# Attention and routed experts on one core: partition sums in four column tiles with a block transpose, and the causal mask as a select on GpSimd

## The reference, cut to what matters

```
q, k, v = (x @ w.T) reshaped to heads            # 16 heads, 128 wide
q, k = rmsnorm(q, q_norm_w), rmsnorm(k, k_norm_w) # x * rsqrt(mean(x*x) + 1e-6) * w
q, k = apply_rope(q), apply_rope(k)
scores = 50 * tanh(q @ k.T / sqrt(128) / 50)
scores = where(mask above the diagonal, -inf, scores)
attn = softmax(scores)
x = layernorm(x + (attn @ v) @ wo.T)
x = layernorm(x + moe(x))                         # 32 experts, 6 per token, and a shared one
```

## Time and profile before

| | |
|---|---|
| runs | 1281.82, 1280.22, 1281.23 us; median 1281.23 |
| profiled execution, span from first to last instruction | 1275.8 us |
| what lies around the span (median less span) | 5.4 us |
| TensorE, VectorE, ScalarE, GpSimd busy over the span | 1137.5, 1077.5, 700.1, 745.7 us |
| mean granted TensorE clock | 0.976 of full speed |
| one step of the attention, mean of 31 | 30.26 us |

### The profile page before, as it was taken

The page is one execution under the profiler, slowest core; times in us unless marked ns, Lnnn a source line. Parts: engine busy times, 40 slices in busy tenths (PEclk is TensorE's granted clock), DMA queues, the critical chain, the costliest instruction groups (busy, mean ns, idle before and its releaser), DMA issues.

```text
span 1275.8 us, 21790 instructions
## 1 busy us (share of the span) xinstructions
PE 1137.5 (89%) x6879; PEld 963.6 (76%) x6879; DVE 1077.5 (84%) x1683; ACT 700.1 (55%) x1143; POOL 745.7 (58%) x665
## 2 busy tenths in 40 slices
PE   4699999989999999999999999999988878499998
PEld 3578788878888887888888888788877753277788
DVE  5599999999999999999999999999999669814654
ACT  2466666666666666666666666666666523022210
POOL 2366767676666666676667676767677536170001
PEclk9799999999999999999999999999999879799999
DMA  4000100000000000000000011100000070017911
GB/s 149 26 31 25 47 21 29 21 29 21 29 25 25 25 25 25 25 25 25 25 25 25 25 32 33 33 21 29 21 21 17 1 237 1 0 50 199 240 33 54
DMA packets 42142, 55.67 MB, mean 44 GB/s; under 512 B 8864, under 2 KB 34816, under 8 KB 42112
## 3 DMA queue, kind: packets, MB, share of 16 engines
q1 hardware_dynamic: 36336, 49.49, 12.8%
q10 hardware_dynamic: 5200, 4.22, 1.2%
q0 software_dynamic: 576, 1.57, 0.4%
HBM read 49.37 MB, written 4.33 MB: 42 GB/s over the span
## 4 chain that ended last, share of the span: by engine, by line
PE 33%; POOL 26%; DVE 22%; issue 11%; ACT 5%; DMA 2%; POOLq 1%; SPq 0%; DVEq 0%; ACTq 0%
POOL rstd L870 10%; POOL pacc L891 9%; PE ps L358 7%; POOL praw L881 6%; PE ps L360 6%; PE ps L359 6%; DVE qraw L1098 6%; DVE qhat_lo L1015 5%; PE ps L615 3%; PE ps L623 2%; ACT praw L711 2%; DVE qhat_hi L1025 2%; ACT prob_hi L672 2%; PE ps L640 2%; PE ps L641 2%
## 5 line engine op out<-in xcount | busy, mean ns | idle before, releaser
L881 POOL TENSOR_TENSOR praw<-praw,causal 128x128 f32<-128x128 f32 x256 | 211.9, 828 | 236.8 <-ACT praw L711 236.8
L672 ACT ACTIVATE prob_hi<-praw 128x1024 fp32r<-128x1024 f32 (+7 forms) x256 | 171.3, 683 | 216.6 <-POOL praw L881 216.5
L1015 DVE TENSOR_TENSOR prob_lo<-praw,prob_hi 128x1024 fp32r<-128x1024 f32 (+7 forms) x256 | 256.1, 1020 | 38.0 <-ACT prob_hi L672 36.8
L891 POOL TENSOR_TENSOR pacc<-pacc,praw 128x768 f32<-128x768 f32 (+2 forms) x192 | 239.3, 1247 | 28.5 <-POOL praw L881 26.6
L358 PE MATMUL ps<-qhat_hi,kT_hi 128*128 128x512 f32 (+3 forms) x384 | 144.6, 376 | 66.5 <-DVE qhat_lo L1015 42.7
L705 ACT ACTIVATE praw<-ps,rstd 128x1024 f32<-128x1024 f32 (+7 forms) x256 | 182.8, 735 | 11.8 <-PE ps L360 3.0
L711 ACT ACTIVATE praw<-praw 128x1024 f32<-128x1024 f32 (+7 forms) x256 | 163.4, 677 | 0.0
L870 POOL TENSOR_TENSOR rstd<-var,mhalf 128x16 f32<-128x16 f32 x32 | 125.3, 3915 | 60.7 <-DVE var L1053 60.7
L358 PEld LDWEIGHTS ps<-qhat_hi,kT_hi 128*128 128x128 f32 x384 | 73.4, 191 | 93.3 <-issue 40.3
L358 PE MATMUL ps<-prob_hi,vS_hi 128*128 128x512 f32 (+3 forms) x384 | 136.5, 355 | 2.6 <-DVE prob_lo L1015 2.5
L360 PE MATMUL ps<-qhat_hi,kT_lo 128*128 128x512 f32 (+3 forms) x384 | 134.0, 349 | 0.0
(11 more groups left out here) (170 smaller groups left out, 2516.7 us busy)
## 6 DMA issues: line engine op xcount, KB each, us to landing
rqB<-rq_rows SPq DMA_DIRECT2D x32, 512.0 KB, 3.7
wgu<-in_wgu SPq DMA_DIRECT2D x32, 352.0 KB
wd<-in_wd SPq DMA_DIRECT2D x32, 176.0 KB
wraw<-in_wqkv SPq DMA_DIRECT2D x16, 256.0 KB, 3.6
wv<-in_wqkv SPq DMA_DIRECT2D x16, 128.0 KB, 2.1
woraw<-in_wo SPq DMA_DIRECT2D x16, 128.0 KB, 2.0
yacc<-in_x SPq DMA_DIRECT2D x1, 2048.0 KB, 13.9
x_rows<-yacc SPq DMA_DIRECT2D x2, 1024.0 KB, 8.6
```

The source lines that it names most:

```text
L672: return nc.scalar.activation(dst, src, ACT.Copy)
L881: nc.gpsimd.tensor_tensor(diag, diag, causal[:, :], ALU.mult).then_inc(mask_done, 1)
L891: nc.gpsimd.tensor_tensor(pacc[:, b, P * j:T], before, raw, ALU.add).then_inc(pacc_done, 1)
L1015: v.tensor_tensor(dst, x_, hi.bitcast(F32), ALU.subtract).then_inc(done, 1)
```

## The change

The squares are no longer reduced on VectorE before the matmul. TensorE multiplies them as the moving operand with a 128 x 32 stationary operand of ones, 256 columns at a time, in four column tiles of 32 columns: tile g takes the 32-token strips g, g+4, g+8 and so on, and writes PSUM partitions 32g to 32g+31, all 32 rows alike. VectorE then transposes the bank in 32 x 32 blocks, after which column 0 of each block holds 32 tokens' sums down the partitions, and one instruction makes `var` of it. The denominators are made in the same way from `pacc`: four matmuls of 256 columns in place of eight loads of `pacc`, all at one place behind scores 3, and a transpose of 128 x 256 ahead of the reciprocal. `rstd` now has token 128 j + p at (p, j), so the q half is written to DRAM element by element, 4 bytes each. The mask is an `affine_select` in place on the diagonal block. Some constants go or move to the routed part.

```
-                mm(ps[:, bank_no, 0:2 * BLK * TT], fold[:, :], sqp[:, :, :, :].rearrange("p m g j -> p (m g j)"),
-                   start=True, stop=True).then_inc(pj_done, 1)
+            def strip_sums(bank_no, c0, by_strip):
+                for g in range(BLK):
+                    last = mm(ps[32 * g:32 * g + 32, bank_no, c0:c0 + 32 * TT].rearrange("p (j r) -> p j r", r=32), ones[:, :],
+                              by_strip[:, g], start=True, stop=True, tile_position=(0, 32 * g))
+                return last
+            def strips(row):
+                return row.rearrange("p (j g r) -> p g j r", g=BLK, r=32)
...
+                pe.wait_ge(qsq_done, step + 1)
+                strip_sums(bank_no, 0, strips(qsq[:, :]))
+                pe.wait_ge(ksq_done, step * 2 + 2)
+                strip_sums(bank_no, 32 * TT, strips(ksq[:, :])).then_inc(pj_done, 1)
...
+                strip_sums(bank_no, 0, strips(pacc[:, b, :])).then_inc(pj_done, 1)
...
-                sp.dma_start(rq_d[b].rearrange("(p j) -> p j", p=P), rstd[:, b, 0:TT]).then_inc(rq_out, 16)
+                sp.dma_start(rq_d[b].rearrange("(j p) -> p j", p=P), rstd[:, b, 0:TT], allow_slow_non_contiguous=True).then_inc(rq_out, 16)
...
-                nc.gpsimd.tensor_tensor(diag, diag, causal[:, :], ALU.mult).then_inc(mask_done, 1)
+                nc.gpsimd.affine_select(out=diag, in_=diag, compare_op=ALU.is_ge, fill=0.0, base=0,
+                                        pattern=[[1, P]], channel_multiplier=-1).then_inc(mask_done, 1)
...
-                    for g in range(BLK):
...
-                    last.then_inc(pj_free, 1)
+                    v.transpose(sqT[:, :], bank).then_inc(folded, 1)
+                    dve.wait_ge(folded, step + 1)
+                    v.tensor_scalar(var[:, b, :], sqT[:, :].rearrange("p (n r) -> p n r", r=32)[:, :, 0],
+                                    1.0 / DH, RMS_EPS, ALU.mult, ALU.add).then_inc(pj_free, 1)
...
-                v.reciprocal(rsum[:, b, :], ps[:, bank_no, 0:TT]).then_inc(pj_free, 1)
+                v.transpose(sumT[:, :], ps[:, bank_no, 0:32 * TT]).then_inc(pj_free, 1)
+                dve.wait_ge(pj_free, count)
+                v.reciprocal(rsum[:, b, :], sumT[:, :].rearrange("p (j r) -> p j r", r=32)[:, :, 0]).then_inc(rsum_done, 1)
```

More of the change, by code:

```diff
@@ L413, in values, with sums @@
                 last.then_inc(pv_done, 1)
-            def sums(s, b, half, count, bank_no):
-                if half == 0:
-                    open_unit(count)
-                    pe.wait_ge(pacc_done, (s + 1) * TT + RING)
-                for j in range(TT // 2 * half, TT // 2 * half + TT // 2):
-                    last = mm(ps[:, bank_no, j:j + 1], pacc[:, b, P * j:P * j + P], ones[:, 0:1], start=True, stop=True)
-                if half == 1:
-                    last.then_inc(pj_done, 1)
+            def sums(s, b, count, bank_no):
+                open_unit(count)
+                pe.wait_ge(pacc_done, (s + 1) * TT + RING)
+                strip_sums(bank_no, 0, strips(pacc[:, b, :])).then_inc(pj_done, 1)
             def out_proj(s, b, u, count, bank_no):
@@ L470, in step @@
                     values(s - 1, 1 - b, 7)
-                    sums(s - 1, 1 - b, 0, *hd.unit(b, "sums"))
                 scores(s, b, 2)
@@ L474, in step @@
                 if old:
-                    sums(s - 1, 1 - b, 1, *hd.unit(b, "sums"))
+                    sums(s - 1, 1 - b, *hd.unit(b, "sums"))
                     if b == 1:
@@ L512, in _ @@
                 values(s - 1, 1, j)
-            for half in range(2):
-                sums(s - 1, 1, half, *end.unit(0, "sums"))
+            sums(s - 1, 1, *end.unit(0, "sums"))
             for u in range(4):
@@ L676, in _, with squares_free, projected @@
                 copy_hi(xT[0][:, :, b * T:b * T + T], xraw[:, :, b * T:b * T + T]).then_inc(xhi_done, 1)
-            def projected(what, b, count, bank_no):
+            def squares_free(step):
+                if not (isinstance(step, int) and step == 0):
+                    act.wait_ge(folded, step)
+            def projected(what, b, step, count, bank_no):
                 if what == "q":
+                    squares_free(step)
                     act.wait_ge(pj_free, count)
@@ L854, in _ @@
             for row, col, value in ((0, 1, 1.0), (1, 1, float(P)), (2, 2, 1.0)):
[L855 removed]
+                pool.wait_ge(consts, 6 + row)
                 nc.gpsimd.affine_select(out=rest[:, col:col + 1], in_=rest[:, col:col + 1], compare_op=ALU.not_equal, fill=value,
                                  base=-row, pattern=[[0, 1]], channel_multiplier=1).then_inc(consts, 1)
[L858 to L863 removed]
             pool.wait_ge(consts, CONSTS)
@@ L1050, in projected @@
                 if what == "ss":
-                    for g in range(BLK):
-                        rows = slice(32 * g, 32 * g + 32)
-                        last = v.tensor_scalar(var[rows, b, :].rearrange("p (m j) -> p m j", m=2),
-                                               bank[rows, 0:2 * BLK * TT].rearrange("p (m g j) -> p m g j", m=2, g=BLK)[:, :, g, :],
-                                               1.0 / DH, RMS_EPS, ALU.mult, ALU.add)
-                    last.then_inc(pj_free, 1)
+                    v.transpose(sqT[:, :], bank).then_inc(folded, 1)
+                    dve.wait_ge(folded, step + 1)
+                    v.tensor_scalar(var[:, b, :], sqT[:, :].rearrange("p (n r) -> p n r", r=32)[:, :, 0],
+                                    1.0 / DH, RMS_EPS, ALU.mult, ALU.add).then_inc(pj_free, 1)
                     return
@@ L1116, in tile, with out_projected @@
                 lo_of(prob[1][:, j % RING, 0:n], praw[:, j % RING, 0:n], prob[0][:, j % RING, 0:n], plo_done)
-            def out_projected(b, u, sums_count, count, bank_no):
+            def out_projected(b, u, step, count, bank_no):
                 if u == 0:
-                    dve.wait_ge(pj_free, sums_count)
+                    dve.wait_ge(rsum_done, step + 1)
                 dve.wait_ge(pj_done, count)
@@ L1160, in step @@
                     tile(s - 1, 6)
-                if new:
-                    fold_squares(s + 1, 0)
                 if old:
@@ L1173, in step @@
                     output_lo(s - 1)
-                if new:
-                    fold_squares(s + 1, 3)
                 if old:
                     summed(1 - b, *hd.unit(b, "sums"))
-                    out_projected(1 - b, 0, hd.unit(b, "sums")[0], *hd.unit(b, "op0"))
+                    out_projected(1 - b, 0, s - 1, *hd.unit(b, "op0"))
                 if new:
@@ L1182, in step @@
                 if old:
[L1183 removed]
+                    out_projected(1 - b, 1, s - 1, *hd.unit(b, "op1"))
                 tile(s, 1)
@@ L1244, in _ @@
             for u in range(4):
-                out_projected(1, u, end.unit(0, "sums")[0], *end.unit(0, f"op{u}"))
+                out_projected(1, u, s - 1, *end.unit(0, f"op{u}"))
             dve.wait_ge(pj_free, UNITS_ALL)
```

102 lines of the change are left out of this document (30 added, 72 removed).

## The result

The changed kernel takes 1546.61 us (median of 4 runs, 1541.71 to 1547.61), the kernel before 1280.72 (1279.32 to 1281.82, 4 runs) on the same chip: a ratio of 1.206, 95% interval 1.2025 to 1.2098. The forecast was 1287, the range 1243 to 1358. It is slower, as the likeliest case said, but by 266 us where that case had 6, and beyond the range.

A forecast was written before the change was run, and what follows sets the result against it. A latency loop of TensorE, VectorE's var, GpSimd's power and a three-engine tail bounds the kernel: 0.63 - 0.45 = +0.18 us a step, times 31 is +5.6, from 1275.8 to 1281.4, plus 5.4 gives 1287 us; range 1243 to 1358.

The forecast's parts named there:

- the likeliest case: Whole kernel: slower, chance 0.59 in all; the main forecast, chance 0.45, had +0.18 us a step, +5.6 us.
- The transfer: Write of rstd's q half in 1024 packets of 4 bytes: 0.5 us more taken, other bound 10 us; costs nothing.
- the row on packets: Profile's view of transfers: 144 packets at 4.6% of 16 engines over 1.7 us, 8.7 ns each.
- the 1.8 that were free: Slack in us before q's scaling needs the transferred row, after GpSimd's gain from the masks.
- Rival C: 4-byte packets become the bound: from some 37 ns each slack is gone, 60 ns adds 62 us, 1349; chance 0.10.
- the 2.2 that were free: Slack in us between the row's landing at about 585.1 and q's scaling making progress at 587.35.
- The wait ahead of the denominators: TensorE's wait of 0.64 us for a bank VectorE has not yet read, predicted to go.
- The middle way of 5 and 9 passes: TensorE's column-tile matmuls overlap partly: denominators 1.08 us, squares 1.94, plus 0.1 a group; squares end 0.56 later.
- rival A: All four column tiles run at once on TensorE: squares end 0.71 earlier, step 1.09 us shorter, 1247 us; chance 0.20.
- VectorE's part: Squares' end to var 0.17 us longer, 0.1 back on average; the net 5.9 us saved counted at nothing.
- GpSimd's part: Affine select for the mask product: 0.45 us off a step over four masks, bounds 0.16 to 0.64.
- B: Rival: column tiles on TensorE take turns, squares end 2.73 later, +2.35 us a step, 73 us, 1354; chance 0.25.

The follow-up runs named there:

- e1_fixed: The changed kernel with the q half of rstd written in whole 32-byte pieces, q's strips read at a step of 8: 1253.33 us, ratio 0.979.
- e4_product: e1_fixed with the causal mask as a product on GpSimd again instead of the affine select: 1275.59 us, ratio 0.996.
- e12_ss_values7: e1_fixed with the squares' sums on TensorE moved from behind scores 4 to behind values 7, their VectorE transpose also earlier: 1188.28 us, ratio 0.927.
- e9_in_turn: e1_fixed without column tiles, the same strip matmuls each over all 128 columns, keeping only the last strip's sums: 1395.48 us, ratio 1.091.
- e13_order_alone: The kernel before with the affine select, VectorE's fold kept, squares' sums moved behind scores 3, last fold and variances earlier: 1375.14 us, ratio 1.072.

## Why the prediction was wrong, point by point

**The transfer: the step that failed.** I had two bounds for the write: 8.7 ns a packet, from the engines' share, hence +0.5 us, and 175 ns for each of 56 more, from the 1.4 us to landing, hence +10. I took the first, "from the row on packets". It measured 9.2 in place of 1.4, +7.8. The row on packets was right on the packets (7.2 ns) and does not hold the completion, which is what the reader of the row waits for. The bounds were sound for the shown step, the choice between ends that far apart was not: with the dearer bound the prediction's own sum, 10 less the 1.8 that were free, gives 8.2 in a step, 254 us, and some 1541. That this comes so near the measured 1547 is partly luck, as it holds no clock and no slower writes. Rival C, which had this wait, was priced at 60 ns a packet and so reached only +68 us. (Its threshold of 37 ns does not fit its own sum: 65 packets at 37 ns add 2.3 us, not 1.8. Nothing hangs on it.) In the shown step 1.4 us of the write became 9.18 and the read took 5.59 in place of about 4; `rqB` landed 18.66 after the start of `rstd`, against the 9.4 I had worked out. With the 2.2 that were free used up, 7.1 are left; VectorE's faster rounding and subtraction give 0.7 of it back (22.09 from `rstd` to scores 0, against 15.70), and 1.1 come on top up to the next `rstd`. That is 7.5 of the 7.6 by which this step is longer than the mean step before; the mean is 8.3, since most other writes take longer (up to 12.3).

**What the wait did besides.** Scaling and low half ran faster (1.30 and 1.24 in place of 2.26 and 1.92), as GpSimd was done by then. Against that, the first passes after the wait start 0.43 apart in place of 0.23, at a granted clock of 0.50, the 1.2 GHz level, after 7.7 to 7.8 us in which TensorE stood idle. Up to the tenth pass of the step it is 3.73 us (586.88 to 590.61) in place of 2.18 (561.06 to 563.24), so 1.55 are lost. Some 0.55 come back up to the end of the squares, as the next paragraph shows; what is left, with 0.1 more from there to `rstd`, is the 1.1 just named. It is a consequence of the wait and no cause of its own: in e1_fixed the span's mean clock is 0.975, here 0.889.

**TensorE's part.** The wait ahead of the denominators went, as said. The middle way of 5 and 9 passes was wrong: the four tiles run together even with two passes each, 0.57 and 1.00 us, as rival A had it and as the span rule of "TensorE: Matmul & The Clock Gate" of the Trainium skill, Part 3, asks. For going over to tiles and back the rows leave 0.14 a group above 0.43 and 0.86, near the 0.1 I had added. Rival A's 0.71 was nearly there in the changed kernel: the squares end 14.61 into the step that starts at 586.88 (601.49), and less the 1.55 of the clock that is 13.06, against 13.61 before, 0.55 earlier. In e1_fixed they end only 0.10 earlier, because they take 1.47 with the strided q, not 1.00.

**VectorE's part.** One transpose of 128 x 512 from PSUM is 0.72 and the variances 0.18, as taken. In e1_fixed, which has the whole change but the write's order and reads q at a step, `rstd` starts 14.66 into the step, as in the kernel before (14.64), where my sum gave 15.3 (I wrote 15.4). That VectorE's saved time counts next to nothing was right for this order (e4_product: 4 us) and is no property of the saving (e12_ss_values7).

**GpSimd's part.** Right in kind, too small: I took 0.45 us a step. Alone it measured 29 us; the step of its profiled execution, the slowest of the five, is 0.79 shorter (30.26 to 29.47). Some 0.16 came off every mask that was read, the blocked ones too, which was my upper bound, and 0.3 off VectorE's scaling and cast behind them, for which I had nothing.

**Rivals.** A had the tiles right, B is what e9_in_turn shows without tiles, C had the place and the wait right and the price too small. The error in the tiles is small beside that of the write and, if anything, hid a little of it.

## What to carry to other kernels

The time of a small write that somebody waits for is its completion, not its packets: where a new form of it isn't in the trace, take the bound from landing until a run says otherwise, and keep writes whole rather than put many single words side by side. In this kernel the work taken off VectorE counted only once the sums it had freed were moved to where their inputs are ready, and then every queue they pass had to be looked at: 1.5 us of TensorE ahead of values 6 and 7 gave 1251.6 us, the same 1.5 us behind them 1188.3. At the second place `rstd` is also 1 us shorter, and no run separates that from the rest of the difference.

## What the runs showed of the hardware

- 512 writes of 4 bytes side by side take 7.9 to 10.6 us to complete, 1024 that lie 64 bytes apart 2.5 to 3.2, with about the same time of a packet itself (7.7 and 7.2 ns).
- Four fp32 matmuls of 256 columns on four column tiles take 0.57 us, over the whole array in turn 1.54 to 1.56. With a moving operand read 8 elements apart they take 0.91 (587.90 to 588.81 in e1_fixed) and 3.68.
- An affine select of 128 x 128 takes 0.29 where the product takes 0.45, and is some 0.16 shorter also where it stands blocked behind VectorE (1.01 against 1.18, 1.28 against 1.45).
- A GpSimd power of 128 x 16 takes 2.91 us undisturbed and 3.84 to 3.95 where a two-input instruction of VectorE started just ahead of it. An instruction of VectorE that started behind it was not held (1.22 us).
- Where waits left TensorE idle for 7.7 us a step, its next passes ran at a granted clock of 0.50, 0.43 apart in place of 0.23; idle times of at most 1.0 and 0.7 us a step in the kernel before left it at 1.00, and those of 1.9 and 1.3 in e13_order_alone went with 0.87 on average.
